# Softmax attention on one core: two groups of heads weighed into one bank, and negated maxima turned by VectorE in blocks of 32

## The reference

```python
q = (x @ Wq.T + bq).reshape(B, L, H, hd)     # k, v in the same way; B, L, H, hd = 8, 512, 16, 8
q = _apply_rope(q, cos, sin)                 # k too
scores = jnp.einsum('bqhd,bkhd->bhqk', q, k) / np.sqrt(hd).astype(np.float32)
attn = jax.nn.softmax(scores, axis=-1)
out = jnp.einsum('bhqk,bkhd->bqhd', attn, v).reshape(B, L, D)
return out @ Wo.T + bo
```

## Time and profile before

| | us |
|---|---|
| median of three runs | 1555.32 |
| lowest and highest | 1548.15, 1560.02 |
| the profiled execution's own time | 1545.64 |
| its span, first to last instruction | 1543.8 |

### The profile page before, as it was taken

One profiled execution on the slowest core, in us unless ns is written; L12 is line 12 of the kernel. 1 busy time (PEld: TensorE's weight loads), 2 busy tenths in 40 slices (PEclk: granted clock), 3 DMA queues, 4 the chain that ended last, 5 costly groups with the idle time before them and its releaser, 6 DMA issues.

```text
span 1543.8 us, 23348 instructions
## 1 busy us (share of the span) xinstructions
PE 1208.7 (78%) x7329; PEld 798.8 (52%) x7329; DVE 833.3 (54%) x2723; ACT 729.7 (47%) x1494; POOL 727.5 (47%) x968
## 2 busy tenths in 40 slices
PE   3219989689999999999629978725999777469994
PEld 2219878322232322222219967624889656448884
DVE  6542146688898999888222445461223677512124
ACT  3214444167777767677414543422444466324431
POOL 3564755222233535524544555563554357735543
PEclk9999999799999999999759989857999987679997
DMA  9156777744454344241056865433558321135576
GB/s 280 44 148 191 216 217 227 205 133 132 108 152 145 90 141 123 67 143 37 15 142 190 248 194 166 132 117 108 168 169 256 105 75 70 40 108 177 161 237 202
DMA packets 164073, 226.83 MB, mean 147 GB/s; under 512 B 20656, under 2 KB 123440, under 8 KB 163952
## 3 DMA queue, kind: packets, MB, share of 16 engines
q1 hardware_dynamic: 119152, 174.05, 39.1%
q0 software_dynamic: 18304, 37.65, 7.2%
q10 hardware_dynamic: 26496, 13.64, 3.1%
HBM read 152.81 MB, written 72.20 MB: 146 GB/s over the span
## 4 chain that ended last, share of the span: by engine, by line
PE 53%; DVE 14%; issue 11%; DMA 7%; POOL 6%; ACT 3%; SPq 3%; another core or an unknown queue 2%; ACTq 0%; POOLq 0%; DVEq 0%
PE PS L1344 16%; PE PS L1334 16%; PE PS L1443 5%; PE PS L1466 5%; DVE arena L2126 5%; POOL dispatched L706 3%; PE PS L1324 2%; PE PS L1451 2%; DMA arena<-experts 2%; PE PS L1429 1%; POOL dispatched L896 1%; DMA YC<-expert_out 1%; ACT arena L1064 1%; DVE BST L1721 1%
## 5 line engine op out<-in xcount | busy, mean ns | idle before, releaser
L734 POOL DMA_INDIRECT expert_out<-arena x316 | 304.4, 963 | 350.7 <-issue 242.3
L970 ACT ACTIVATE arena<-PS,arena 128x256 f32<-128x256 f32 (+1 forms) x568 | 266.7, 498 | 405.0 <-PE PS L1334 356.7
L1064 ACT ACTIVATE arena<-PS 128x512 f32<-128x512 f32 x512 | 286.2, 596 | 130.1 <-PE PS L1443 121.4
L1334 PE MATMUL PS<-arena 128*128 128x256 f32 (+1 forms) x1136 | 313.4, 418 | 20.9 <-issue 11.2
L1344 PEld LDWEIGHTS PS<-arena 128*128 128x128 f32 x2528 | 311.7, 196 | 25.8 <-issue 10.6
L1344 PE MATMUL PS<-arena 128*128 128x128 f32 x2528 | 315.7, 280 | 8.7 <-DVE arena L1998 7.3
L2126 DVE TENSOR_REDUCE arena<-PS 128x2 f32<-128x1024 f32 x256 | 302.6, 1218 | 21.7 <-PE PS L1453 19.9
L1998 DVE TENSOR_TENSOR arena<-PS,arena 128x256 f32<-128x256 f32 (+1 forms) x142 | 64.5, 454 | 408.1 <-PE PS L1344 312.7
L1334 PEld LDWEIGHTS PS<-arena 128*128 128x128 f32 x1136 | 210.0, 196 | 75.3 <-issue 18.7
L706 POOL DMA_INDIRECT dispatched<-arena x192 | 185.3, 965 | 102.7 <-issue 59.9
L1443 PE MATMUL PS<-arena 96*128 96x512 bf16 x512 | 173.2, 392 | 12.7 <-ACT arena L1064 7.1
(11 more groups left out here) (258 smaller groups left out, 1231.5 us busy)
## 6 DMA issues: line engine op xcount, KB each, us to landing
arena<-experts SPq DMA_DIRECT2D x142, 578.0 KB
qk_products<-arena SPq DMA_DIRECT2D x48, 384.0 KB
arena<-qk_products SPq DMA_DIRECT2D x64, 288.0 KB
arena<-dispatched SPq DMA_DIRECT2D x110, 129.0 KB
dispatched<-FILL SPq DMA_DIRECT2D x32, 322.5 KB
YC<-expert_out ACTq DMA_DIRECT2D x40, 256.0 KB
arena<-qk_products SPq DMA_DIRECT2D x64, 128.0 KB
arena<-dispatched SPq DMA_DIRECT2D x32, 193.5 KB
```

The source lines that it names most:

```text
L734: pool.indirect_dma_start(YK, bass.IndirectOffsetOnAxis(ap=ID[:, s:s + 1], axis=0), YS[:, s, :], None).then_inc(s_yo[r], 16)
L970: act.activation(HT[:, tau % PAIR, q, 0:S * P], hidden_chunk(S, q), func, bias=WE[:, r, 2 * DFF + q:2 * DFF + q + 1]).then_inc(s_g, 1)
L1064: act.activation(PT[:, G % 2, j, k, :], bank(4 + k % 2), ACT.Exp, scale=float(1.0 / np.sqrt(HD))).then_inc(s_exp, 1)
L1334: pe.matmul(hidden_chunk(size(f, tau), q), WE[:, r, q * P:q * P + P], XPT[:, tau % PAIR, 0:N], start=True, stop=True).then_inc(s_h, 1)
```

## The change

The negated maxima are no longer transposed by TensorE and copied by ScalarE. VectorE writes both bf16 parts side by side, 32 columns, and transposes them in four blocks of 32 by 32 into NMT. For this it waits until the maxima rows of the group before have been read. SyncE writes the rows by four DMAs, one for each block, in pieces of 32 numbers in place of 128.

Two groups, 2q and 2q + 1, accumulate into one bank 6. The strip of a head pair has 18 rows: 9 for the head of the even group, 9 for that of the odd. V in VA has 27 columns for a pair of heads: 8 channels, a one, 9 zeros, 8 channels, a one. The even group's weights are columns 0 to 17, the odd group's 9 to 26, so each adds zeros to the other's rows. The copy of bank 6, `turn_values` and the reciprocal then happen once in two groups; the product is done in two halves. VA becomes a ring of 2 batches of the same total size, and `values_front` moves from (g = 0, j = 1) to (g = 1, j = 0) on TensorE and to (g = 1, j = 1) on VectorE, with its addition in two halves.

```diff
-V_RING = 3
+V_RING = 2
+VCOLS = 2 * (HD + 1)
+VPAIR = 3 * (HD + 1)
...
 # SyncE, max_rows(G)
-                    for k in range(2):
-                        sp.dma_start(QS[M_ROW + k:M_ROW + k + 1, r].rearrange("o h (a t) -> o (h a) t", t=P),
-                                     NMT[16 * k:16 * k + 16, :]).then_inc(s_nmi[r], 16)
+                    rows = QS[M_ROW:M_ROW + 2, r].rearrange("o h (a t) -> o (h a) t", t=P)
+                    for n in range(BLOCKS32):
+                        sp.dma_start(rows[:, :, 32 * n:32 * n + 32], NMT[32 * n:32 * n + 32, :]).then_inc(s_nmi[r], 16)
...
 # ScalarE
-                def values(G):
-                    act.wait_ge(s_av, G + 1)
-                    if G > 0:
-                        act.wait_ge(s_tp, G)
+                def values(q):
+                    act.wait_ge(s_av, 2 * q + 2)
+                    if q > 0:
+                        act.wait_ge(s_tp, q)
                     act.activation(OT[:, :], bank(6), ACT.Copy).then_inc(s_ot, 1)
-                def negmax(G):
-                    act.wait_ge(s_nmp, G + 1)
-                    if G > 0:
-                        act.wait_ge(s_nmi[(G - 1) % QK_RING], 32 * ((G - 1) // QK_RING + 1))
-                    act.activation(NMT[0:32, :], bank(7, 0, P)[0:32, :], ACT.Copy).then_inc(s_nmt, 1)
...
-                    if j == 3 and 0 <= G - 1 < GROUPS:
-                        values(G - 1)
+                    if j == 3 and 0 <= G - 1 < GROUPS and G % 2 == 0:
+                        values(G // 2 - 1)
...
 # TensorE, weigh(G, k), with q, o = G // 2, G % 2
-                        if G > 0:
-                            pe.wait_ge(s_ot, G)
-                        else:
+                        if G == 0:
                             pe.wait_ge(s_av0, 1)
+                        elif o == 0:
+                            pe.wait_ge(s_ot, q)
...
-                        mm = pe.matmul(bank(6)[32 * j:32 * j + HD + 1, :], VA[:, G // 4 % V_RING * GT + k, G % 4 * 4 + j, :],
-                                       PT[:, G % 2, j, k, :], start=(k == 0), stop=(k == GT - 1))
+                        mm = pe.matmul(bank(6)[32 * j:32 * j + VCOLS, :],
+                                       VA[:, G // 4 % V_RING * GT + k, q % 2, j, (HD + 1) * o:(HD + 1) * o + VCOLS],
+                                       PT[:, G % 2, j, k, :], start=(o == 0 and k == 0), stop=(o == 1 and k == GT - 1))
...
-                def negmax(G):
-                    pe.wait_ge(s_nmf, G + 1)
-                    pe.transpose(bank(7, 0, P)[0:32, :], NMF.rearrange("p a b -> p (a b)"), ident)\
-                        .then_inc(s_nmp, 1)
...
-                    if j == 1 and g == 0 and batch(b + 1) and b + 1 > 0:
+                    if j == 0 and g == 1 and batch(b + 1) and b + 1 > 0:
                         pe.wait_ge(*read)
                         values_front(b + 1)
...
-                    if j == 0 and 0 <= G + 1 < GROUPS:
+                    if j == 1 and 0 <= G - 2 < GROUPS and G % 2 == 1:
                         pe.wait_ge(*read)
-                        negmax(G + 1)
-                        read = (s_nmt, G + 2)
-                    if j == 1 and 0 <= G - 2 < GROUPS:
-                        pe.wait_ge(*read)
-                        turn_values(G - 2)
-                        read = (s_td, G - 1)
+                        turn_values((G - 2) // 2)
+                        read = (s_td, (G - 2) // 2 + 1)
...
 # VectorE, negmax(G)
+                    chain(dve.tensor_scalar(NMB[:, 0, :], mx, -1.0, None, ALU.mult))
+                    chain(dve.scalar_tensor_tensor(out=NMB[:, 1, :], in0=mx, scalar=-1.0, in1=NMB[:, 0, :],
+                                                   op0=ALU.mult, op1=ALU.subtract))
                     if G > 0:
-                        dve.wait_ge(s_nmp, G)
-                    chain(dve.tensor_scalar(NMB[:, :], mx, -1.0, None, ALU.mult))
-                    chain(dve.tensor_copy(NMF[:, 0, :], NMB[:, :]))
-                    dve.scalar_tensor_tensor(out=NMF[:, 1, :], in0=mx, scalar=-1.0, in1=NMB[:, :],
-                                             op0=ALU.mult, op1=ALU.subtract).then_inc(s_nmf, 1)
+                        dve.wait_ge(s_nmi[(G - 1) % QK_RING], 16 * BLOCKS32 * ((G - 1) // QK_RING + 1))
+                    dve.transpose(NMT[:, :], NMB.rearrange("p k c -> p (k c)")).then_inc(s_nmt, 1)
...
 # VectorE, normalised(q)
+                    chain(dve.reciprocal(RD[:, :, :, :], sums[:, :, :, :, HD]))
+                    if q % 2 == 0 and q >= 2:
+                        dve.wait_ge(s_ap, q // 2)
+                    for o in range(2):
+                        ins = dve.tensor_tensor(heads[:, :, :, o], sums[:, :, :, o, 0:HD],
+                                                RD[:, :, :, o].unsqueeze(3).to_broadcast((P, GT, 4, HD)), ALU.mult)
+                    ins.then_inc(s_td, 1)
...
+BLOCKS32 = P // 32
```

More of the change, by code:

```diff
@@ L243, in build @@
         KH = cv([HI_RING, 2, SEQ], BF16)
-        VA = cv([V_RING * GT, HEADS, HD + 1])
+        VA = cv([V_RING * GT, 2, 4, VPAIR])
         MX = cv([2, 4, GT])
-        NMB = cv([4 * GT], BF16)
-        NMF = cv([2, 4 * GT])
-        NMT = cv([P], BF16)
+        NMB = cv([2, 4 * GT], BF16)
+        NMT = cv([8 * GT], BF16)
         OT = cv([SEQ])
-        RD = cv([GT, 4])
+        RD = cv([GT, 4, 2])
         AO = cv([GT, D])
@@ L1089, in step @@
                         out_rows(b - 1)
-                    if j == 1 and 0 <= G + 1 < GROUPS:
-                        negmax(G + 1)
                     if has_e:
@@ new lines, in negmax, with normalised @@
+                    dve.transpose(NMT[:, :], NMB.rearrange("p k c -> p (k c)")).then_inc(s_nmt, 1)
+                def normalised(q):
+                    sums = bank(7).rearrange("p (a j w) -> p a j w", a=GT, j=4)[:, :, :, 0:VCOLS]\
+                                  .rearrange("p a j (o r) -> p a j o r", o=2)
+                    heads = AO.rearrange("p a (q o j d) -> p a j q o d", q=2, o=2, j=4)[:, :, :, q % 2]
+                    dve.wait_ge(s_tp, q + 1)
+                    chain(dve.reciprocal(RD[:, :, :, :], sums[:, :, :, :, HD]))
+                    if q % 2 == 0 and q >= 2:
+                        dve.wait_ge(s_ap, q // 2)
+                    for o in range(2):
+                        ins = dve.tensor_tensor(heads[:, :, :, o], sums[:, :, :, o, 0:HD],
+                                                RD[:, :, :, o].unsqueeze(3).to_broadcast((P, GT, 4, HD)), ALU.mult)
+                    ins.then_inc(s_td, 1)
@@ L2191, in step @@
                     has_m = 0 <= G + AHEAD < GROUPS
-                    if j == 1 and g == 0 and batch(b + 1) and b + 1 > 0:
+                    if j == 1 and g == 1 and batch(b + 1) and b + 1 > 0:
                         values_front(b + 1)
@@ L2210, in step @@
                         maxima(G + AHEAD, j, 0)
-                    if j == 1 and 0 <= G - 2 < GROUPS:
-                        normalised(G - 2)
+                    if j == 1 and 0 <= G - 2 < GROUPS and G % 2 == 1:
+                        normalised((G - 2) // 2)
                     if has_m:
@@ L2223, in attention @@
                 dve.memset(bank(6), 0.0).then_inc(s_av0, 1)
-                chain(dve.memset(VA[:, :, :, HD:HD + 1], 1.0))
+                ones = VA.rearrange("p t q j c -> p (t q j) c")
+                chain.many(dve.memset(ones[:, :, HD + 1:VCOLS], 0.0),
+                           dve.memset(ones[:, :, HD:VPAIR:VCOLS], 1.0))
                 for G in range(4 - EARLY, GROUPS + LATE):
```

33 lines of the change are left out of this document (12 added, 21 removed).

## The result

| | kernel before | changed kernel |
|---|---|---|
| median of the runs, us | 1557.88 (12 runs, 1548.15 to 1564.08) | 1548.95 (12 runs, 1544.92 to 1554.67) |
| ratio, 95% interval | | 0.9949 (0.9927 to 0.9971) |
| profiled execution, us (span) | 1545.64 (1543.8) | 1546.16 (1544.3) |
| instructions of TensorE / ScalarE | 7329 / 1494 | 7233 / 1446 |

The medians are 8.9 us apart; 8 us had been forecast for the difference and 1547 us for the time. Two later sets of runs, on two chips, gave 0.9922 (0.9898 to 0.9945) and 0.9933 (0.991 to 0.9957). So the change makes the kernel faster by 0.5 to 0.8%. The two profiled executions show nothing of it in their spans: 1543.8 and 1544.3 us. The stage has to be read by itself.

What follows compares the result with a forecast made beforehand. In attention TensorE is busiest (95%), with the bounding engine varying by step. Batches 2 to 5 -5.2, batches 0, 1 and 6 -3.0, batch 7 -1.0, allowance +1: -8.2 us, so 1555.3 - 8 = 1547 us; range 1538 to 1560.

Steps and rivals of the forecast that it cites:

- the slack: In each plain attention step TensorE has 0.46 us to spare; only work exceeding it lengthens the step.
- Plain steps: Attention steps, numbered (group G, j) and timed weigh to weigh, without extra work such as turn_values; said to stay 2.87 us.
- all of TensorE's work counts: Rival, chance 0.13: all removed TensorE turns and transpositions count in full, -19.6 us, giving 1536 us.
- nothing is left: Rival, chance 0.22: VectorE's fuller step and the store chain eat the gain; 1553 to 1556 us.
- the rows land late: Rival, chance 0.10: after g = 1 the four transfers of 64-byte pieces land late; 1567 us at 4 us later.
- (12, 1) 4.10 to 2.87, a gain of 1.23: Group 12, step j = 1: loses both values_front and turn_values, so 1.23 us shorter.
- (13, 0) gains 0.57: Group 13, step j = 0: receives values_front, 1.03 us less 0.46 of slack, so 0.57 us longer.
- The allowance of 0.15 a batch: VectorE's halved addition costs more and turn_values waits for it: 0.15 us in 7 batches, +1 us.
- -0.54 in the late stretch: Around (10, 1), where VectorE is late: the division at G = 10 moves to G = 11, saving 0.54 us.
- Nothing on balance: Transposing the maxima on VectorE instead of TensorE: 0.2 us replaces a 0.22 us cast, so no net gain.
- The rows: +0.5 us, bounds 0 and 1.4: Behind g = 1, four maxima-row DMAs instead of two land 0.5 us later, between 0 and 1.4.
- Batch 7: -1.0: Last batch: two turns at 0.20 us and two copies at 0.21 saved, a little more at low clock: -1.0 us.

Runs made afterwards that it cites:

- four_dummies: Changed kernel with four unread 128x32 TensorE transpositions added at j = 0 in every group but g = 1; 1458.64 us in one execution.
- add_early: Changed kernel with VectorE's addition of values_front moved between the two reductions of (g = 1, j = 0); ratio to the kernel before 0.9971.
- turn_rows_g1: Kernel before with only the maxima turned by VectorE, and their rows sent ahead of the stacks' loads at g = 1; 1544.71 us, ratio 0.992.
- before_again: The kernel before, no edit, profiled a second time; 1560.83 us in one execution.
- turn_only: Kernel before with only the maxima turned by VectorE and their rows sent by four DMAs; 1550.32 us, ratio 0.996.
- pairs_only: Changed kernel with the maxima transposed by TensorE, copied by ScalarE and sent by two DMAs, as before; 1572.74 us, ratio to the kernel before 1.0096.
- move_only: Kernel before with only values_front moved from g = 0 to g = 1; 1580.5 us, ratio 1.0137.
- rows_ahead_g1: Changed kernel with the maxima rows sent ahead of the stacks' loads at g = 1 alone; 1544.85 us, ratio to the kernel before 0.9921.
- after_again: The changed kernel, no edit, profiled a second time; 1543.56 us, ratio to the kernel before 0.9922.

## Why the prediction was right, and where its parts were not

The time came within 2 us of the forecast, and the slack that the argument rests on is shown by four_dummies. But the 8 us were booked to the wrong parts, and that their sum came out near is luck. By batches the forecast, its allowance included, had about -0.9 us each in 0, 1 and 6, -1.2 each in 2 to 5, and -1.0 in 7; the first pair of profiles has -1.7, 0.0 and -1.9, then -0.3, -0.3, -0.8 and -0.7, and -5.7.

*Right.* Plain steps stay 2.87 us. Step (28, 1) lost 0.20. The block transposition took 0.212 us (0.2 said), its wait is covered. The logits' step (10, 0) fell by 0.10 (0.28 at most was said), the extra columns of weights cost nothing (weigh takes 1.05 us with 9 and with 18). The tail passes the gain on: GpSimd, whose row of the changed kernel answers to the earlier trace rows,

```profile
749.14 0.25 POOL L883 TENSOR_TENSOR arena<-arena,CST 128x32 f32<-128x32 f32 x1 [6.93 <-ACT arena L1049]
```

starts 6.5 us earlier than at 755.67, and from there its last transfer is issued at the same distance as before (38.3 us against 38.6). The three rivals did not come: not "all of TensorE's work counts" (four_dummies, and plain steps of 2.87 us), not "nothing is left", not "the rows land late".

*"(12, 1) 4.10 to 2.87, a gain of 1.23".* 3.00 it was, and (12, 2) went from 2.87 to 3.16. ScalarE's two split copies fall into these two steps. Its timeline in the changed kernel:

```profile
480.02 1.06 ACT L1037 ACTIVATE arena<-arena 128x1024 bf16<-128x1024 f32 x1
480.97 2.17 ACT L1065 ACTIVATE arena<-PS 128x512 f32<-128x512 f32 x4
483.19 1.06 ACT L1041 ACTIVATE arena<-arena 128x1024 bf16<-128x1024 f32 x1
484.15 2.15 ACT L1065 ACTIVATE arena<-PS 128x512 f32<-128x512 f32 x4
486.56 0.60 ACT L1065 ACTIVATE arena<-PS 128x512 f32<-128x512 f32 x1 [0.26 <-PE PS L1436]
```

Ahead of each row of this stretch there is no idle time until 486.56: ScalarE sets (12, 1) and (12, 2). In the kernel before it still had pauses of 0.51 and 0.43 us there, since values_front made TensorE the later one. So it seems that values_front covered the copies, and that they show when it goes. That is read from the traces; no experiment moved the copies. The two steps together gained 0.81 and not 1.23.

*"(13, 0) gains 0.57".* 0.63. *The allowance of 0.15 a batch* for the halved addition, the reciprocal (0.348 us, 0.25 said) and the rest was too small: (13, 1) was to stay at 3.07 us and took 3.44, +0.37, and add_early shows that an earlier addition does not help, because VectorE's own work is late there.

*"-0.54 in the late stretch".* (10, 1) to (10, 3) went from 12.39 to 463.45 - 451.43 = 12.02 us: -0.37. Together, batches 2 and 3 gained 0.32 us each instead of 1.3. In batches 4 and 5 group 17 grew from 13.04 to 14.87 us ((17, 2) alone from 3.98 to 4.84), while (18, 1) fell from 5.36 to 3.59. The traces name what pushes (17, 2): TensorE's turn of the attention output waits for VectorE's product, in the kernel before and in the changed kernel

```profile
552.07 0.66 PE L1500 MATMUL PS<-CST,arena 128*128 128x128 f32 x4 [0.62 <-DVE arena L2147]
...
555.40 0.66 PE L1490 MATMUL PS<-CST,arena 128*128 128x128 f32 x4 [1.47 <-DVE arena L2138]
```

and this wait grew by 0.85 us. VectorE works without a pause ahead of it, and the moved addition, 0.75 us, is now in that row of work. In add_early, where the addition comes earlier, (17, 2) takes 4.52 us and (17, 1) as much more, 3.77 for 3.45.

*"Nothing on balance" for the turn.* This failed. Alone the turn has a ratio of 0.996, about half of the gain of the whole change on that chip, and with the rows sent ahead at g = 1 it has 0.992. First, three steps lost 0.8 us each, 0.54 with the step behind, since TensorE no longer waits for VectorE's negated maxima in them. Second, without the turn the move and the pairs cost 15 us and more: the forecast added up the parts as if each stood alone, and never asked what the moved values_front would do to the next reader of bank 7. Third, turn_rows_g1 has the whole gain without pairs or move; how much of it is the order of the rows is open.

*The rows: +0.5 us, bounds 0 and 1.4.* Four issues take 2.69 us, 1.47 more than two (1.2 said). In the changed kernel, SyncE's row and the landing in the chain of waits, batch 1:

```profile
389.05 2.69 SPq L663 DMA_DIRECT2D arena<-arena  x4
```

```profile
381.02 6.04 DMA qk_products<-arena
...
391.13 2.90 DMA arena<-arena
```

The rows land 394.03 - 389.05 = 4.98 us behind the first issue, against 4.36 in the kernel before (385.46 to 389.82): 0.6 later, as forecast. From the end of the last issue it is 2.29 us against 3.14: the longer issue is enough to explain it, and no cost of the small pieces shows. The rule of the Trainium skill that the prediction weighed ("DMA: Bandwidth & Descriptors", Specifications) speaks of transfers below 512 bytes. The pieces before, 256 bytes, and those after, 64, both lie below that, so these rows do not test the rule; they show only that the step from one to the other added nothing that can be seen.

The stores ahead of the rows took 6.04 us to land, where 5.03 was seen in the first profile of the kernel before, and (5, 3) lasts 0.93 us more. That is not the change's doing. The chain of waits of before_again, at the same place, has

```profile
384.61 6.11 DMA qk_products<-arena
```

and (5, 3) lasts 5.58 us and (6, 0) 4.29 there. With stores as late, the changed kernel has 4.32 and 2.92 us in these two steps, and turn_only (6.35 us) 6.00 and 4.72. So where the rows come late, pairs and move seem to be worth something: TensorE waits 1.06 us for the rows in the changed kernel and keeps its clock (granted 1.00), and waits 2.33 us in each of the other two, with the clock at 0.50 behind it. That rests on one place in five profiles. It may be why the whole change (0.9922) beats turn_only (0.996) on the same chip, though their intervals overlap; once the rows are sent ahead of the loads, no difference is left (0.9921 and 0.992). Why the stores land later in one execution than in another is open.

*Batch 7: -1.0.* It was -5.7. The turns and copies are in it with 0.2 in (28, 1) and 0.6 in (31, 3); (30, 1) grew by 0.5; the rest is the clock and a gap. In the kernel before TensorE has two gaps at (30, 1):

```profile
730.78 0.66 PE L1479 MATMUL PS<-CST,arena 128*128 128x128 f32 x4 [0.91 <-issue]
...
734.87 0.88 PE L1443 MATMUL PS<-arena 96*128 96x512 bf16 x2 [2.02 <-ACT arena L1064]
```

and the granted clock is 0.50 from 736 to 748 us; (30, 2) to (31, 1) last 5.18, 4.19, 4.16 and 4.26 us. In the changed kernel the one gap there,

```profile
730.92 0.39 PE L1436 MATMUL PS<-arena 96*128 96x512 bf16 x1 [1.90 <-issue]
```

is followed by full clock, and the same steps last 3.42, 3.13, 2.88 and 2.87: 17.79 us became 12.30, 5.5 less. Of that 12.61 - 8.88 = 3.7 us are in the last three, by the clock. The prediction had kept 3 us for it, outside the sum. Two profiles of the kernel before have the fall here and three of the changed kernel have not; turn_only, pairs_only and move_only have it for 4 to 7 us, turn_rows_g1 and rows_ahead_g1 not. On the second chip no profile has the gap at all: (30, 1) lasts 3.50 us there. So half of what the first pair of profiles shows hangs on a gap and on the clock. Where the gap ends with VectorE's residual, as in before_again, move_only and turn_only, or with "issue", as in the changed kernel, the profile gives no engine that VectorE or TensorE had waited for. The cause of the gaps is open, and with it whether the change has a part in keeping the clock.

So two errors met: the pairs and the move were credited with the whole gain, of which they seem to bring some only where the rows come late, and the turn and the clock with nothing.

## What to carry to other kernels

Read the idle column of a small instruction, not its duration alone: 0.28 us of work was worth 0.8 us in its step, and 0.54 with the step behind, where the engine stood waiting for its input. When an engine's shared bank passes from reader to reader, each edit moves the wait of whoever comes next in that bank, so cost two edits together as well as apart; here the turn is worth -7 us, the move +23, and both with the pairs -9 to -14. A sum that comes out right says little on its terms: time each part alone before keeping the complicated one.

## What was not expected of the hardware

The same kernel took 1463.95 us on one chip and 1557.04 to 1557.88 us in the other sets of runs. In the kernels profiled on the first the difference is not in attention: their plain steps are 2.87 us as elsewhere and the stretch is as long, while what stands ahead of step (1, 0) and behind step (32, 0) is shorter (add_early 282.05 and 757.1 us, after_again 325.02 and 790.5).

A gap does not decide by its length whether TensorE's clock falls. In move_only the same transposition waits 2.83 or 2.84 us seven times; behind the wait that ends at 398.06 us the granted clock is 1.00 (398.1 to 401.1 us), behind the one that ends at 455.30 it is 0.50 (455.4 to 458.4), and (5, 1) lasts 3.07 us but (9, 1) 3.96. Gaps of 1.90 and 2.23 us at step (30, 1) left the clock at 1.00 in the changed kernel and in turn_rows_g1; behind one of 2.02 us in the kernel before, with one of 0.91 us ahead of it, and behind one of 3.10 us in before_again, it was at 0.50 for 12 and 10 us. A gap of 1.47 us in (17, 2) left it at 1.00 in two profiles of the changed kernel and was followed by 0.61 and 0.53 (557 to 561 us) in the third. After a gap of 2.69 us TensorE's eight weigh matmuls took 1.73 us instead of 1.05.

In batch 1 of the changed kernel SyncE needs 0.61 to 0.68 us for each of the four rows' issues, whose transfer holds 2 KB, and 0.32 to 0.60 for the loads of the stacks, which hold up to 288 KB.
